# One fused transformer block: the start of the kernel is reordered (class token, first patch group, loads)

## The reference

```
tokens = einsum('bpi,hi->bph', patches, W) + b
h = concat([class_token, tokens]) * pos_embed ; h = concat([h, txt])      # 16 x 193 x 128
xn = layernorm(h); qk = xn @ Wqk + bqk; q, k = elu(q)+1, elu(k)+1
kv = rope(k)^T xn ; out = rope(q) kv / (q . mean(k)) + depthwise_conv3(xn) ; h = h + out
xn = layernorm(h); shared = silu(xn @ sw1) * (xn @ sw3) @ sw2
h = h + shared + sum over the top 2 of 8 experts of p_e * (silu(xn @ w1_e) * (xn @ w3_e)) @ w2_e
```

## Time and profile before

| | us |
|---|---|
| median of the runs shown | 314.88 |
| the three runs | 306.6, 314.88, 316.8 |
| the profiled execution, its own time | 308.57 |
| its span, first to last instruction | 306.7 |
| mean granted TensorE clock | 0.934 of full |

### The profile page before, as it was taken

One profiled execution on the slowest core, in us unless ns is written; L12 is line 12 of the kernel. 1 busy time (PEld: TensorE's weight loads), 2 busy tenths in 40 slices (PEclk: granted clock), 3 DMA queues, 4 the chain that ended last, 5 costly groups with the idle time before them and its releaser, 6 DMA issues.

```text
span 306.7 us, 5987 instructions
## 1 busy us (share of the span) xinstructions
PE 243.9 (80%) x1489; PEld 194.2 (63%) x1490; DVE 191.8 (63%) x698; ACT 151.7 (49%) x438; POOL 114.2 (37%) x121
## 2 busy tenths in 40 slices
PE   0779799999999996999779589798898998995000
PEld 0648598878888884866556467676676776774000
DVE  1523987969788697586568855555555654542195
ACT  0234476757667585475324125554554544546072
POOL 0300000437373553717450006365465564656100
PEclk9987999999999999599999979999999999999555
DMA  7999713325060101101101122222222222210596
GB/s 225 340 306 343 242 19 141 109 102 182 27 211 18 46 17 34 38 17 43 38 28 44 44 62 77 64 77 63 59 72 65 69 79 69 66 41 20 144 297 180
DMA packets 31413, 31.61 MB, mean 103 GB/s; under 512 B 4322, under 2 KB 27275, under 8 KB 30496
## 3 DMA queue, kind: packets, MB, share of 16 engines
q1 hardware_dynamic: 25128, 23.55, 25.6%
q0 software_dynamic: 3392, 6.36, 6.1%
q10 hardware_dynamic: 2872, 1.45, 1.7%
HBM read 22.82 MB, written 9.03 MB: 104 GB/s over the span
## 4 chain that ended last, share of the span: by engine, by line
PE 56%; DVE 18%; issue 7%; another core or an unknown queue 5%; ACT 5%; DMA 3%; ACTq 2%; SPq 1%; POOLq 0%; POOL 0%; DVEq 0%
PE bank L1448 12%; PE bank L1468 7%; PE bank L1201 6%; PE bank L1186 6%; PE bank L1457 3%; PE bank L1382 3%; PE bank L1269 2%; DMA xd<-y_dram 2%; DVE sh_h L1003 2%; PE bank L1273 2%; PE bank L1256 2%; PE bank L1369 2%; PE bank L1439 2%; PE bank L1370 1%
## 5 line engine op out<-in xcount | busy, mean ns | idle before, releaser
L730 POOL DMA_INDIRECT xs_dram<-xd,pos_i x50 | 55.6, 1113 | 87.1 <-DVE pos_i L915 74.3
L746 POOL DMA_INDIRECT y_dram<-att,goal x56 | 55.1, 985 | 71.3 <-ACT att L675 59.2
L1121 DVE CAST xsT_h<-bank 128x128 fp32r<-128x128 f32 x56 | 16.3, 291 | 45.0 <-PE bank L1439 37.5
L1468 PE MATMUL bank<-w_sb,att 128*128 x224 | 36.1, 284 | 5.0 <-ACT att L663 4.7
L1186 PE MATMUL bank<-wt,xp_both 128*128 128x128 f32 x288 | 39.0, 291 | 0.0
L1186 PEld LDWEIGHTS bank<-wt,xp_both 128*128 128x128 f32 x288 | 37.9, 206 | 1.3 <-issue 0.4
L1468 PEld LDWEIGHTS bank<-w_sb,att 128*128 128x128 f32 x224 | 29.3, 191 | 7.8 <-issue 7.1
L656 ACT ACTIVATE att<-bank 128x256 f32<-128x256 f32 x56 | 21.9, 391 | 21.4 <-PE bank L1448 17.3
L663 ACT COPY att<-bank 128x256 f32<-128x256 f32 x56 | 21.0, 375 | 18.9 <-remote 14.0
L1448 PE MATMUL bank<-xp_both,xsT_h 128*128 x56 | 27.5, 491 | 1.0 <-issue 0.6
L1457 PE MATMUL bank<-cst,att 128*128 128x128 f32 x112 | 22.3, 281 | 5.6 <-DVE att L1140 4.4
(11 more groups left out here) (199 smaller groups left out, 494.9 us busy)
## 6 DMA issues: line engine op xcount, KB each, us to landing
xp_both<-in_patches SPq DMA_DIRECT2D x7, 1152.0 KB
xs<-xs_dram SPq DMA_DIRECT2D x56, 64.5 KB
xd<-y_dram SPq DMA_DIRECT2D x8, 384.0 KB, 6.3
w<-in_w SPq DMA_DIRECT2D x2, 1024.0 KB, 9.5
y_dram<-att,goal POOLq DMA_INDIRECT x56
xs_dram<-xd,pos_i POOLq DMA_INDIRECT x50
hrow<-in_txt SPq DMA_DIRECT2D x2, 384.0 KB, 10.6
wt<-in_w_tok SPq DMA_DIRECT2D x2, 320.0 KB, 5.8
```

Source lines behind the costliest of these rows:

```text
L730: nc.gpsimd.indirect_dma_start(out=xs_dram[:, :], out_offset=bass.IndirectOffsetOnAxis(ap=pos_i[0:rows, j, k:k + 1], axis=0), in_=xd[0:row ...
L746: nc.gpsimd.indirect_dma_start(out=y_dram[:, :], out_offset=bass.IndirectOffsetOnAxis(ap=goal[u][:, 0:1].bitcast(I32), axis=0), in_=ys[u][ ...
L1468: last = M(bank[6 + q][:, 0:D], hmT[q][:, m, :], w[:, bass.ds(first + m * D, D)], start=(m == 0), stop=(m == 1))
```

## The change

On SP, one wait is added: the texts `hrow[:, 4:6]`, and all that stands behind them in SP's stream (the patches of group 1, the other texts), are issued only when the third piece of the first weights and patches has landed. On ACT, the small transfer of `bqk` and two texts move ahead of `wqk`, and three transfers (`cols`, `gateb_sb`, `dest_sb`) go to POOL's queue. On PE, tokens(0, 0) and (0, 1) come ahead of the class's transpose, and tokens(0, 2) and (0, 3) ahead of its `wqk` product. The transposes and product of `ft_c` move behind `turn_rows(0)`, as `turn_class`. In the first iteration the third tile is projected ahead of tokens(1, 0). ACT takes the class's exponential behind `norm_patches(0)`, and DVE makes `ft_c` behind `mean1(0)`, and `kv_c` behind the texts' statistics.

```
 (SP)
             sp.dma_start(xr[0][0:KR, :], patches[KB * P:IN_D, :]).then_inc(s_wtok, 16)
+            sp.wait_ge(first_loaded[2], 32)
             sp.dma_start(hrow[:, 4:6, :], txt[2:4]...).then_inc(txt_loaded[1], 16)
 (ACT)
+            act.dma_start(bq_in[:], ...)                       # ahead of cst
             act.dma_start(cst[:], consts[:, :]).then_inc(s_cst, 16)
+            act.dma_start(hrow[:, 1:3, :], ...)                # ahead of wqk
             act.dma_start(wqk_sb[:], wqk[:, :]).then_inc(s_wqk, 16)
-            act.dma_start(bq_in[:], ...)
             act.dma_start(posb[:], pos[1:1 + P, :]).then_inc(s_pos, 16)
-            act.dma_start(hrow[:, 1:3, :], ...)
-            act.dma_start(cols[:], ...); gateb_sb; dest_sb     # now pool.dma_start, behind the memsets
...
-            act.wait_ge(cls_pe, C_QK)                          # was ahead of the loop
-            A(ex_c[:], bank[1][0:B, 0:2 * D], ACT.Exp, bias=-1.0).then_inc(cls_act, 1)
-            act.wait_ge(s_cols, 32)
                     norm_patches(i + 1)
+                if i < 0:
+                    act.wait_ge(cls_pe, C_QK)
+                    A(ex_c[:], bank[1][0:B, 0:2 * D], ACT.Exp, bias=-1.0).then_inc(cls_act, 1)
+                    act.wait_ge(s_cols, 32)
 (DVE)
-            dve.wait_ge(s_cst, 16)                             # now behind the five splits of bq
...
             patch_stats(0)
+            mean1(0)
+            dve.wait_ge(cls_act, C_EX)
+            V.scalar_tensor_tensor(out=ft_c[:], ...).then_inc(cls_dve, 1)
+            text_stats(1)
             dve.wait_ge(cls_pe, C_KV)
             V.tensor_tensor(kv_c[:], bank[5][:, 0:D], mask, ALU.mult).then_inc(cls_dve, 1)
-            mean1(0)
-            text_stats(1)
 (PE)
+            tokens(0, 0)
+            tokens(0, 1)
             pe.wait_ge(s_cst, 16)
             pe.wait_ge(cls_act, C_ROW)
             T(bank[6][:, 0:B], xcls[:], ident[0:B, 0:B]).then_inc(cls_pe, 1)
-            tokens(0, 0)
-            tokens(0, 1)
+            tokens(0, 2)
+            tokens(0, 3)
...
             M(bank[1][0:B, 0:2 * D], xclsT[:], wqk_sb[:], start=False, stop=True).then_inc(cls_pe, 1)
-            tokens(0, 2)
-            tokens(0, 3)
...
                 turn_rows(i)
+                if i == 0:
+                    turn_class()
                 if i >= 1:
                     attend(i - 1)
                 project_most(i)
+                if i == 0:
+                    project_rest(i)
                 if i + 1 < G:
                     tokens(i + 1, 0)
                 if i >= 1:
                     mixed_rows(i - 1)
-                project_rest(i)
+                    project_rest(i)
```

More of the change, by code:

```diff
@@ L419, in _ @@
             act.dma_start(cls_in[:, 1, :], pos[0:1, :].broadcast_to([B, D])).then_inc(s_cls, 16)
+            act.dma_start(bq_in[:], bqk[:, :].broadcast_to([4, 2 * D])).then_inc(s_bq, 16)
             act.dma_start(cst[:], consts[:, :]).then_inc(s_cst, 16)
+            act.dma_start(hrow[:, 1:3, :], txt[0:2].rearrange("b t d -> t b d")).then_inc(txt_loaded[0], 16)
             act.dma_start(wqk_sb[:], wqk[:, :]).then_inc(s_wqk, 16)
-            act.dma_start(bq_in[:], bqk[:, :].broadcast_to([4, 2 * D])).then_inc(s_bq, 16)
             act.dma_start(posb[:], pos[1:1 + P, :]).then_inc(s_pos, 16)
[L424 to L427, removed]
             act.preload_act_table_set("natural_log_exp_and_others")
@@ L705, in _ @@
             nc.gpsimd.memset(pad[:], 0.0).then_inc(pad_set, 1)
+            pool.dma_start(cols[:], small[:, :]).then_inc(s_cols, 16)
+            pool.dma_start(gateb_sb[:], gate_b[:, :].broadcast_to([P, E])).then_inc(s_cols, 16)
+            pool.dma_start(dest_sb[:], dests[:, :]).then_inc(s_ids, 16)
             pool.wait_ge(s_cst, 16)
@@ L933, in _ @@
             then(V.tensor_copy(bq_h[:, 2, :], bq_part[:, 1, :]))
+            dve.wait_ge(s_cst, 16)
             then(V.tensor_scalar(bq_sel[:, 0, :], bq_h[:, 0, :], split[:, 0:1], split[:, 3:4], ALU.mult, ALU.add))
@@ L942, in _ @@
             text_stats(0)
-            dve.wait_ge(cls_act, C_EX)
-            V.scalar_tensor_tensor(out=ft_c[:], in0=ex_c[:], scalar=1.0, in1=bank[1][0:B, 0:2 * D],
-                                   op0=ALU.min, op1=ALU.max).then_inc(cls_dve, 1)
             mean_texts(1, 0, 1)
@@ L949, in _ @@
             patch_stats(0)
+            mean1(0)
+            dve.wait_ge(cls_act, C_EX)
+            V.scalar_tensor_tensor(out=ft_c[:], in0=ex_c[:], scalar=1.0, in1=bank[1][0:B, 0:2 * D],
+                                   op0=ALU.min, op1=ALU.max).then_inc(cls_dve, 1)
+            text_stats(1)
             dve.wait_ge(cls_pe, C_KV)
             V.tensor_tensor(kv_c[:], bank[5][:, 0:D], mask, ALU.mult).then_inc(cls_dve, 1)
-            mean1(0)
-            text_stats(1)
             dve.wait_ge(turns_set, 6)
@@ L1319, in _, with turn_class @@
             M(bank[1][0:B, 0:2 * D], xclsT[:], wqk_sb[:], start=False, stop=True).then_inc(cls_pe, 1)
-            tokens(0, 2)
-            tokens(0, 3)
[L1322 to L1326, removed]
+            def turn_class():
+                pe.wait_ge(cls_dve, C_FT)
+                for i in range(2):
+                    last = T(bank[6][:, 32 * (1 + i):32 * (1 + i) + B], ft_c[:, D * i:D * i + D], ident[0:B, 0:B])
+                last.then_inc(cls_pe, 1)
+                M(bank[5][:, 0:D], ft_c[0:1, D:2 * D], xcls[0:1, :], start=True, stop=True).then_inc(cls_pe, 1)
             pe.wait_ge(small_set, 4)
```

## The result

The changed kernel took 314.50 us in the median of four runs (313.27 to 316.34), the kernel before 311.85 in the median of its four (306.6 to 316.8). The ratio given with it is 1.0226, with a 95% interval from 1.0115 to 1.0336: slower, where 313.4 and a gain were forecast, though the interval doesn't tell whether by 2%. That ratio leaves out runs over 1.5% above the fastest of the same kernel, so all four of the changed kernel stand against 306.6 and 308.81 alone. By the medians of all four the changed kernel is 0.8% above. The experiments show what this does to a comparison.

What follows compares the result with a forecast made beforehand. A chain over all engines, PE above all, was taken as the bound, with PE waiting at the start for the class token. 2.0 - 0.1 - 0.4 + 0 = 1.5 us off 314.88 gave 313.4, range 304.0 to 317.0.

Steps and rivals of the forecast that it cites:

- Part 1: Start on PE: patches ahead of the class token, piece 1 landing unchanged at 9.4; gain 1.4 to 2.5, taken as 2.0 us.
- 10.5 as a sign of being wrong: First patches: piece 1 landing at 8 or at 10.5, where 9.4 us was taken, would make the prediction wrong.
- Part 3: Start, three small transfers moved to POOL's queue: cost 0 to 0.65 us on piece 1, taken as 0.1.
- Rival (c): First patches: ACT's queue still runs beside them and POOL's come earlier, costing piece 1 0.65; 313.9 us, chance 0.15.
- Part 2: SP's wait ahead of group 1's patches and texts: piece 3 up to 1.6 us earlier, gain 0, patches still in time.
- rival (d): Group 1: its patches come too late, landing after 23 us; 3 us of loss, 316.4 us, chance 0.03.
- Part 4: Class token's second half on PE, behind the normalized rows: costs 0.3 to 0.5 us, taken as 0.4.
- Part 5: First iteration, third tile projected first: a swap of the same PE work, gain 0, at most 0.1 us.
- (a): PE's clock stays up through the idle stretch behind the first patch product: 3 us more gain, 310.4 us, chance 0.20.
- (b): PE's clock stays low from the start through group 1, whose matmuls lose 2.1 us: 316.0 us, chance 0.12.
- The attention and scatter stages of later groups should look as before, shifted: Group loop behind the start: later stages unchanged, only shifted by 1.5 us.
- The level: Whole run: the old median of 314.88 us moved by the same 1.5 us gain as the profiled execution, to 313.4.

Runs made afterwards that it cites:

- e9: The changed kernel, unchanged, run again on chip A beside the kernel before: median 312.90 us, ratio 1.0208.
- e17: The changed kernel, unchanged, run again on a B chip (number 12) beside the kernel before: median 286.03 us, ratio 0.9981.
- e16: The changed kernel with the old loads on SP and ACT (the order alone), on a B chip (number 13): 284.25 us, ratio 0.9922 to the kernel before.
- e3: The changed kernel with the old loads (no SP wait, ACT issues all ten), on chip A: 307.71 us, ratio 1.0024 to the kernel before.
- e6: The changed kernel without the wait on SP, on a B chip (number 8): 286.62 us, ratio 0.9962 to the kernel before.
- e2: The kernel before with only the loads changed (SP's wait, ACT's order, three transfers on GpSimd), on chip A: 315.35 us, ratio 1.0296.
- e1: The kernel before, without any edit, timed against itself on chip A: 314.09 us, ratio 1.0234.
- e11: The changed kernel with the three small loads back on ACT, on chip A: median 308.37 us, ratio 0.9923 to the kernel before.
- e10: The kernel before, unchanged, timed against itself again on chip A: median 311.96 us, ratio 1.0165.
- e13: The kernel before with only the three small loads moved to GpSimd, on a B chip (number 13): 285.89 us, ratio 1.0016.

## Why the prediction was wrong, point by point

**Part 1, "I take that landing as it was".** This is the step of the sum that failed. PE's first matmul came at 4.15 (4.2 forecast) and the eight matmuls took 2.07 (1.7). Piece 1 landed 8.5 us after its issue and not 7.3, in seven profiles of kernels that have ACT's new order and the three loads on GpSimd 7.9 to 8.9. In the changed kernel's profile it landed at 10.6, and the prediction had named 10.5 as a sign of being wrong. The 2.0 us of gain came out as 0.0 in the changed kernel's profile; in e9 the first product ended at 16.69 and in e17 at 16.16. Five profiles of the kernel before, or of it with later scatters, ended it between 17.4 and 18.5. The means are 16.7 and 17.9, a gain near 1. The 7.3 was itself one draw: in these five profiles piece 1 took 6.6 to 8.0.

The price of the matmuls was the smaller half of the miss. From PE's resuming to the end of the product were 6.67 us in this profile, 6.26 in e9 and 5.55 in e17, where the forecast ran from 5.5 to 6.6. The names "cold" and "warm", TensorE's clock at its lower and its higher level, are not what the rows show: the granted clock is 1.00 in every window of the kernel before up to 20 us, and of the changed one up to 19.5, those in which matmuls cost 0.21 to 0.26 us as well as those in which they cost 0.13. The price at a granted 0.50 is 0.21 too (ten matmuls in 2.13 us from 23.73), so the prices were near and the reason given for them is open.

**Part 3, 0.1 us for the small transfers.** I had the bound of 0.65 and took the low end, because "only part can fall there". With ACT's new order they cost about 2 us on piece 1 (7.9 to 8.9 with them, mean 8.5 of seven profiles; 6.1 to 7.0 without them, mean 6.5 of five), more than their share of engine time in the earlier trace rows. Against the kernel before the landing is only 1.0 later in the mean (8.5 and 7.5), since the other changed loads bring piece 1 forward: with PE's new order and all the old loads it takes 7.5 and 7.6 (e16, e3), against that 6.5. I put this down to ACT's new order and not to SP's wait, which e6 without it doesn't show (8.6). The two were not tried apart without the loads on GpSimd. Rival (c), at 0.15, was the true case of the start, at a higher price than its 0.65: ScalarE's and GpSimd's queues run beside the first patches, and nothing had the engines to itself. The Trainium skill's DMA: Bandwidth & Descriptors (queues, rings and completion order) says that each DMA engine goes round-robin between the queues that have work. The trace agrees in direction: piece 1 landed later with a third queue at work, 8.5 against 6.5 us.

**Part 2, the wait on SP: gain 0.** Right. e6 without it has the same landings, and a time whose ratio to the kernel before (0.9962) lies within the interval of e17's. The wait ended later than forecast, with the patches of group 1 issued at 13.18 and not at 11 to 12, but they were there in time (PE has no wait at 25.52), so rival (d) is out.

**Part 4, 0.4 us for `turn_class`.** Right in size: from the end of the first product to the first projection 21.21 - 17.37 = 3.84, where it was 20.72 - 17.39 = 3.33, 0.5 more, part of it at the lower clock.

**Part 5, gain 0.** Right. The rotation's products end at 28.07 + 0.95 = 29.02 us, and DVE then waits 3.2 us for the patch product of group 1, until 32.2.

**Rivals (a) and (b), the clock.** (a) didn't come: the idle stretch was followed by the lower level. Nor did (b) as it was written, since the granted clock was 1.00 from the start to 19.5. But the lower level lasted 10.2 us, and group 1's 36 matmuls took 6.24 us in place of 5.5, a third of (b)'s 2.1. This isn't a property of the change: the step from group 0 to group 1 took 14.8, 12.0 and 13.6 us in three profiles of the changed kernel, and 13.3, 11.9 and 13.4 in three of the kernel before. It moves by 1.5 to 3 us from run to run with either.

**"The attention and scatter stages of later groups should look as before, shifted".** This step failed too, and it is what turned the sign in the measurement. I had no rival for it. On chip A every profile with the loads on GpSimd and unheld scatters has steps of 14.7 us, with late counts beside the scatters (e2, e9). Without these loads some have them (e1, e11) and some have 13.3 (e3, e10). The trace of before had the marks: a division that waited 1.47 us for no releaser of the core at 64.77, and an exponential on ACT that waited 2.64 us at 66.19 for products done at 64.80. I read only the first 36 us and the chain's totals. I also wrote that I didn't know where the 6.3 us between the profiled execution and the median lay, and took them as a constant. Most of them are four steps of the loop that take 13.3 or 14.7 us: between e1's profile (314.49) and this one they differ by 58.3 - 53.3 = 5.0 us, and what stands behind them by 1.2 more. And in both profiles of the changed kernel outside the B chips, the steps were long.

**The level.** The median of 314.5 lies 1.1 from the forecast 313.4, but by two errors: the start gained less than forecast, and the time is not the old median with a gain on top but the upper of two rhythms.

## What to carry to other kernels

A transfer of few bytes in small packets on a further queue isn't free while the first pieces are awaited: keep it behind them in a queue that is in use, and judge by landings whether they have the engines to themselves. When the runs of one program spread by 3%, find the place in the trace that has two lengths before pricing anything, time the kernel against itself, and compare medians of all runs. Read what waits beside scatters issued by GpSimd: a chain that PE's other work just hides in one profile is open by 1.5 us in the next.

## What the runs showed of the hardware

- On chip A, with GpSimd's indirect scatters in flight, instructions on ACT and DVE that wait for a count of PE start up to 2.7 us behind the matmul's end; with no scatter beside the loop the same waits are 0.4 us at most. On three other chips the changed kernel, the kernel before with the loads moved, and their variants show none of it. The kernel before takes 311.8 us on A and 285.7 to 286.1 on those three in the median, 8% less.
- A late count lasts until about 1.1 us behind the end of a scatter's issue (81.39 against 80.26), in e9 1.0 and in e3 1.1. Once a group is late, those behind it are late too (that the delay moves the next scatters onto the next denominators is my reading of the rows; no run forced it). Steps are 13.2 to 13.4 or 14.7 to 14.9, with one or two between when it starts.
- Three transfers of 6, 4 and 25.5 KB issued by GpSimd at 1.4 to 3.2 us put off the landing of a 320 KB piece by 2.0 us in the mean of twelve profiles, 0.9 at the least, where ACT's queue has its new order. On the old order the one profile (e13, 8.0) lies at the upper end of the 6.6 to 8.0 without them. Issuing them took GpSimd 0.73, 0.58 and 0.54 us.
